# Selective-scan stage of a conv/attention/MoE block: ring sizes for C rows, decays and POOL inputs

## What is computed

```python
dA = jnp.exp(d_t[..., None] * As)                       # decay, one per state n of 16
h = h * dA + (d_t * u_t)[..., None] * B_t[:, :, None, :]  # the scan along 1024 positions
y = jnp.einsum('bkcn,bkn->bkc', h, C_t)                 # read-out: sum over n of h * C
# four directions k: rows, columns, and both reversed; 192 channels; batch 4
```

## Time and profile before

| | before |
|---|---|
| median of runs | 2733.45 us |
| the profiled execution | 2734.34 us, of which the span is 2732.6 us |
| scan stage (24 halves) | about 269 to 1637 us |
| busy in 269 to 1637 us | DVE 1252.9, POOL 1267.8, PE 1089.5, ACT 873.9 us |
| granted TensorE clock there | 0.90 of 2.4 GHz |

### The profile page before, as it was taken

The page is one execution under the profiler, slowest core; times in us unless marked ns, Lnnn a source line. Parts: engine busy times, 40 slices in busy tenths (PEclk is TensorE's granted clock), DMA queues, the critical chain, the costliest instruction groups (busy, mean ns, idle before and its releaser), DMA issues.

```text
span 2732.6 us, 21603 instructions
## 1 busy us (share of the span) xinstructions
PE 2204.3 (81%) x6116; PEld 1010.2 (37%) x6116; DVE 1603.2 (59%) x1337; ACT 1150.1 (42%) x1277; POOL 1440.8 (53%) x503
## 2 busy tenths in 40 slices
PE   4885877787887887887777886779898559999998
PEld 1332332333333333333323332345455325555554
DVE  2434899999899998899999896742212200000000
ACT  1225666666666666666666663211111011111111
POOL 0001998999999999999899995000000231111111
PEclk9997899988899889899989898789999679999999
DMA  5116121112111121112112213101101342232220
GB/s 197 58 23 152 52 62 47 54 54 71 54 54 54 54 71 54 54 54 54 54 46 61 55 53 155 41 35 47 46 0 46 121 165 103 107 107 101 107 103 17
DMA packets 69131, 193.92 MB, mean 71 GB/s; under 512 B 10160, under 2 KB 35875, under 8 KB 67426
## 3 DMA queue, kind: packets, MB, share of 16 engines
q1 hardware_dynamic: 62946, 176.45, 21.0%
q0 software_dynamic: 6144, 16.98, 1.8%
HBM read 154.89 MB, written 40.44 MB: 71 GB/s over the span
## 4 chain that ended last, share of the span: by engine, by line
PE 46%; DVE 21%; issue 17%; POOL 9%; ACT 4%; DMA 1%; SPq 1%; DVEq 1%; POOLq 0%; ACTq 0%
PE ps L1079 9%; PE ps L1067 9%; DVE arena L1228 7%; PE ps L843 6%; POOL arena L462 6%; DVE ps L1221 5%; PE ps L787 3%; PE ps L824 3%; DVE arena L1186 3%; PE ps L1031 3%; PE ps L956 2%; POOL arena L436 2%; PE ps L798 2%; DVE arena L1181 2%; PE ps L832 2%
## 5 line engine op out<-in xcount | busy, mean ns | idle before, releaser
L462 POOL TENSOR_TENSOR arena<-arena 128x2048 f32<-128x2048 f32 x192 | 901.6, 4701 | 97.6 <-DVE arena L1228 85.4
L843 PE MATMUL ps<-arena 128*128 128x512 f32 x1536 | 803.1, 649 | 14.5 <-DVE arena L1198 14.5
L824 PE MATMUL ps<-arena 96*128 (+1 forms) x1248 | 383.4, 418 | 282.0 <-DVE arena L1228 159.6
L1228 DVE TENSOR_TENSOR_SCAN arena<-arena,ps 128x1024 f32<-128x1024 f32 x240 | 548.8, 2287 | 40.9 <-DVE ps L1221 33.0
L618 ACT ACTIVATE arena<-ps 128x1024 f32<-128x1024 f32 x384 | 392.1, 1021 | 424.8 <-PE ps L824 268.8
L843 PEld LDWEIGHTS ps<-arena 128*128 128x128 f32 x1536 | 319.2, 208 | 299.1 <-issue 226.2
L443 POOL TENSOR_TENSOR arena<-arena 128x1024 f32<-128x1024 f32 x144 | 361.9, 2514 | 2.9 <-POOL arena L436 1.9
L824 PEld LDWEIGHTS ps<-arena 96*128 96x128 bf16 x1248 | 113.5, 104 | 648.6 <-DVE arena L1228 244.7
L1228 DVE TENSOR_TENSOR_SCAN arena<-ps,arena 128x1024 f32<-128x1024 f32 x144 | 327.9, 2277 | 26.5 <-ACT ps L610 26.4
L1221 DVE TENSOR_TENSOR ps<-ps,arena 128x1024 f32<-128x1024 f32 x240 | 291.7, 1215 | 50.6 <-PE ps L824 48.1
L1445 DVE TENSOR_TENSOR arena<-ps,arena 128x384 f32<-128x384 f32 x32 | 17.9, 558 | 448.8 <-PE ps L1079 448.8
(11 more groups left out here) (167 smaller groups left out, 1865.5 us busy)
## 6 DMA issues: line engine op xcount, KB each, us to landing
arena<-b_rows SPq DMA_DIRECT2D x288, 256.0 KB, 3.9
arena<-in_w SPq DMA_DIRECT2D x16, 2304.0 KB, 13.3
slot_in<-arena SPq DMA_DIRECT2D x8, 772.0 KB, 16.5
arena<-slot_in SPq DMA_DIRECT2D x8, 772.0 KB, 17.9
arena<-in_xT SPq DMA_DIRECT2D x4, 1536.0 KB, 9.0
arena<-in_x_tok SPq DMA_DIRECT2D x1, 6144.0 KB, 22.1
tokens<-arena SPq DMA_DIRECT2D x4, 1536.0 KB, 5.8
out<-arena SPq DMA_DIRECT2D x4, 1536.0 KB, 9.7
```

Of the source, the lines that this page charges most:

```text
L462: nc.gpsimd.tensor_tensor(hst[:, h:h + 2], hst[:, h:h + 2], c_sb[:, c:c + 2], ALU.mult).then_inc(p2_ok, 2)
L824: mm = pe.matmul(dst[:, h * 512:(h + 1) * 512], sel_lhs[0:BR, n], bc[0:BR, q % OJ // J, dr, m, h * 512:(h + 1) * 512], start=True, stop=True)
L843: mm = pe.matmul(Y_PS[:, h * 512:(h + 1) * 512], ident, hst[:, u % HRING, h * 512:(h + 1) * 512], start=(u == 0), stop=(u == UN - 1))
L1228: nc.vector.tensor_tensor_scan(h, f, x, 0.0, ALU.mult, ALU.add).then_inc(sc_ok, 1)
```

## The change

`RING` now counts the C rows alone, and there are eight slots for them. The decays get a ring of their own, `DRING` = 2, whose slot is counted by the DVE states alone; the exp waits for the scan of the DVE state two before (`decay_before`). `XRING` goes from four to two. The space is the same: with the 8 slots of `hst`, 20 slots of 1024 columns before (decays 4, C rows 4, inputs 4) and after (2, 8, 2). No instruction is added or removed.

```diff
-RING = 4
+RING = 8
+DRING = 2
-XRING = 4
+XRING = 2
+def decay_slot(u):
+    return (u - pool_units(u)) % DRING
+def decay_before(u):
+    vec = [v for v in range(-UN, UN) if v % UN not in POOL_UNITS]
+    return vec[vec.index(u) - DRING]
...
-        dlt, dux, decay = rs.take(2, S), rs.take(2, S), rs.take(RING, S)
+        dlt, dux, decay = rs.take(2, S), rs.take(2, S), rs.take(DRING, S)
...
-                    kept = 2 if n in ON_POOL else RING
-                    dst = B_PS[u % 2] if n in ON_POOL else decay[:, u % RING]
-                    if not (first and u < kept):
-                        act.wait_ge(sc_ok, U + (3 - kept))
+                    held = u - 2 if n in ON_POOL else decay_before(u)
+                    dst = B_PS[u % 2] if n in ON_POOL else decay[:, decay_slot(u)]
+                    if not (first and held < 0):
+                        act.wait_ge(sc_ok, q * UN + (held + 3))
...
-                        f, x = decay[:, u % RING], slot
+                        f, x = decay[:, decay_slot(u)], slot
```

More of the change, by code:

```diff
@@ L87 @@
 VEC_UNITS = UN - len(POOL_UNITS)
+assert VEC_UNITS % DRING == 0
+def decay_slot(u):
[3 more added lines that the diff above has]
+    return vec[vec.index(u) - DRING]
 assert len(POOL_UNITS) % XRING == 0
```

## The result

The changed kernel takes 2710.91 us (median of six runs, 2709.20 to 2715.63) against 2734.16 us for the kernel before in the same runs: a ratio of 0.9916 [0.9898, 0.9933], 0.8% faster. The forecast was 2826 us and slower, with a range of 2730 to 2890 us. The profiled execution took 2710.37 us with a span of 2708.6 us. Lines have moved by 14: the scan is L1242, the product L1235, the three delta steps L1195, L1200, L1205 (before: L1181, L1186, L1191), the read-out L476, the input L457, the exp L624, the C copy L632, the spreads L838, the addition of y L857.

What follows compares the result with a forecast made beforehand. DVE and POOL alternate in the scan stage, neither saturated; the change was to make POOL fix each half. 22 halves +82 us, first half +8, late landings and starts +2, on 2734.3 us: 2826 us, range 2730 to 2890.

Steps and rivals of the forecast that it cites:

- What bounds the kernel: Scan stage: DVE and POOL alternate, neither saturated; a half averages 59.01 us, and one losing less at its start becomes longer.
- the C ring: DVE's waits at units 1 to 4 fall from 3.3 us, gaining 1.4 to 3.0 us per half if nothing else moved.
- The decay ring at 0: Exps of DVE states wait for an earlier scan, but the scan they feed comes 5 us or more later: cost 0.
- `XRING` = 2 makes the collision the rule: Read-out (4,5) ends 11.3 us after scan 4, so L1181 is issued 0.8 to 2.0 us before that in 23 halves.
- the collision: DVE's first delta step, L1181, is issued while POOL still runs read-out (4,5), with (6,7) queued behind.
- the sum: Halves of 62.74 instead of 59.01 us: 22 give +82 us, first half +8, late DMA landings and input starts +2.
- The price: What a colliding L1181 loses: between nothing and 7.2 us plus what POOL has left of read-out (4,5).
- the long value: L1181 waits until POOL runs dry: 7.2 us plus the rest of read-out (4,5); taken from two rows of 8.40 us.
- the short value: Lower bound at L1181: nothing lost, if DVE gets in at the end of the running read-out.
- The difference that I named: At L1186 input 14 was queued before DVE asked; at L1181 read-out (6,7) and input 12 are queued after.
- DVE gets in at the first boundary: Rival: L1181 starts as read-out (4,5) ends, halves of 56.6 us, 2684 us (2670 to 2705); chance 0.19.
- The rule of the Trainium skill: DVE and POOL lock a shared port pair for one whole instruction, so L1181 would lose only one read-out's rest.

Runs made afterwards that it cites:

- b_drain: Kernel before, with POOL also waiting for its own input 9 ahead of read-out (4,5), a pause of 0.29 us: 2727.69 us, ratio 0.9961.
- c_drain: Changed kernel with four input slots again, and POOL also waiting for its own input 9 ahead of read-out (4,5): 2694.31 us, ratio 0.9853.
- d_only: Kernel before with only the new ring of two decay slots; four C slots and four input slots: 2738.09 us, ratio 1.0014.
- c_only: Changed kernel with four input slots again, eight C slots and two decay slots kept: 2767.64 us, ratio 1.0099.
- one_op: Changed kernel with the first delta step reading one SBUF operand instead of two: 2708.30 us, ratio 0.9896.

## Why the forecast was wrong, step by step

- *What bounds the kernel; the C ring.* Right. The gain is on DVE's waits at units 1 to 4, C copies no longer wait for POOL, and PE's addition at n = 1 is what is late next. With the pause in both, the C ring with the decay ring takes a half from 58.70 (b_drain) to 57.13 us (c_drain), 1.57 us, within the 1.4 to 3.0 us that were worked out.
- *The decay ring at 0.* Right (d_only, 1.0014).
- *`XRING` = 2 makes the collision the rule.* Right: forecast leads of 0.8 to 2.0 us in 23 halves, measured 0.91 to 2.80; read-out (4,5) ends 11.3 us after scan 4 by the forecast, 11.3 to 12.1 us by the trace. The C ring alone would have made it nearly the rule (19 of 23 in c_only). But the sum put nothing on the B row itself, because read-out (4,5) was put at 39.6 us into the half. In nine halves it ends at 41.7 to 42.5 us. This is the term of the sum that was left out, worth 9 x (58.86 - 57.02) = 17 us. I had written 1.9 us of DVE waits at 1.2 GHz for these halves and then not carried them through scan 4 to the B row.
- *The price.* This step failed: "I take the long value: the two rows with this very sequence show it". The runs showed the short value: L1195 came out 1.1 us after the end of the running read-out in all 23 halves, after 2.0 to 3.9 us, where 8.4 us and more had been priced. The sequence was the same, the history was not. In both rows of before POOL had run eight instructions without a pause (the earlier trace rows begin with read-out (4,5), which stands right behind them), and in the kernel after it pauses for B row 9, one instruction before (4,5), by the very wait that I had found: 4.5 us after scan 4. I used that wait to place the collision and not to ask what it does to POOL. The 82 us of the forecast hang on this. Two cases of an outcome with an unknown condition were taken for a rule, against 23 rows of L1186 in the same trace.
- *The difference that I named* (which instruction is queued first) does not decide: 190 steps got in ahead of a read-out queued no earlier than they asked.
- *The rival that came true* is "DVE gets in at the first boundary", which had a chance of 0.19: L1195 at 2.0 to 3.9 us, first half +2. Its own range, 2670 to 2705 us, missed the measured time by 6 us, and L1186 was the right precedent for it without the reason being known. It gave 2684 us, 26 below the profiled execution. Of that the long halves are 9 x (58.86 - 56.6) = 20 us, the short ones 13 x (57.02 - 56.6) = 5, and the work behind the last marker 1.
- *The rule of the Trainium skill* ("SBUF — State Buffer", section "SBUF: two separate sides"), an exclusive lock for one whole instruction, describes the 190 steps that came out right behind the running read-out, after their own work alone (1.1 us, in one_op 0.55). It does not describe the 35 that stayed out over several POOL instructions, for 8.4 to 10.8 us.

What made the change faster is then this. The C ring is worth 1.57 us a half with the pause in both kernels, but it brings scan 7 forward into read-out (4,5), and with four input slots 14 of 23 halves lose over 5 us by that (c_only, +33 us in all). The input ring of two costs 57.77 - 57.13 = 0.64 us a half (changed kernel against c_drain; 58.03 - 57.13 = 0.90 with the pause in both), and its wait breaks POOL's run at the right place. Nothing in the change was aimed at that pause; that it falls there is luck. A gain of 23 us stands where 40 are to be had.

**Open.** Why the chance of being shut out grows with POOL's run is not shown; nor whether instructions or time count (each takes 2.4 or 4.5 us), nor why a DVE step, once out, is never let in before POOL is dry, nor why the second step never is. What makes PE's addition slow after one idle time of 2.2 us and not after another is open too. In c_only four of four steps with a lead of 0.3 us got in after eight instructions, while four with 0.5 to 0.6 us in the kernel before and in d_only did not; lead may matter beside the run, and no run varied it alone.

## What to carry to other kernels

When DVE steps that read and write SBUF fall into a dense stream of POOL instructions, look in the timeline for single DVE steps that are many times their usual length and end where POOL runs dry; if they are there, a POOL pause of 0.3 us just before (a wait on its own last result is enough) is worth trying before any reordering. When a trace shows one event with two prices, find what differs in the history of the engines before it, and do not take the price from the rows that merely have the same neighbours. A wait that a change adds must be carried through to everything it moves: here it placed a collision, cured it, and delayed a read-out, and only the first was in the sum.

## What the hardware showed unexpectedly

- A DVE step on SBUF can stay shut out past the running POOL instruction and two more: 8.4 to 10.8 us, 25 of 38 times after eight without a pause, 0 of 151 after none or one. A pause of 0.07 us was enough (13 halves of the changed kernel paused 0.07 to 0.54 us).
- A semaphore wait of POOL on its own previous instruction leaves it idle for 0.29 us.
- A tensor_scalar on 128x1024 f32 with one SBUF operand took 0.69 us (a two-operand step 1.20) and waited for POOL in 23 of 23 collisions, as the two-operand step did.
- After PE had idled 2.0 to 2.3 us its next four f32 matmuls took 2.81 to 3.68 us in nine halves of the changed kernel, and 1.98 us in four: the idle time alone does not decide.
